# Adding one full-size product ahead of each set of 27-row products in the merging of the feed-forward weights

## The reference, cut to what matters

```python
gh = relu(einsum('bsd,hd->bsh', x, gfc1_w) + gfc1_b)
g = (einsum('bsh,eh->bse', gh, gfc2_w) + gfc2_b).mean(axis=1)   # 32 samples x 8
W1m = W1 + einsum('be,efd->bfd', g, tv_W1)                      # 32 x 512 x 128
W2m = W2 + einsum('be,edf->bdf', g, tv_W2)                      # 32 x 128 x 512
h = relu(einsum('bsd,bfd->bsf', x, W1m) + b1m[:, None, :])
out = einsum('bsf,bdf->bsd', h, W2m) + b2m[:, None, :]
```

## Time and profile before

| | |
|---|---|
| median of 3 runs | 759.09 us (758.73 to 762.13) |
| the profiled execution | 757.8 us, its span 755.8 us |
| busy, share of the span | TensorE 84%, weight loads 72%, VectorE 68%, ScalarE 58%, GpSimd 43% |
| mean granted TensorE clock | 0.912 of full speed |
| the merging, first to last product | 143.7 to 180.1 us |

### The profile page before, as it was taken

How to read it: one execution, slowest core, us unless ns; L and a number is a source line. 1 busy time by engine, 2 the same in 40 slices (tenths; PEclk the granted TensorE clock), 3 DMA queues, 4 the chain that set the end, 5 groups by cost and what they waited for, 6 DMA issues and landing times.

```text
span 755.8 us, 17403 instructions
## 1 busy us (share of the span) xinstructions
PE 637.0 (84%) x5635; PEld 540.7 (72%) x5635; DVE 511.3 (68%) x1393; ACT 437.7 (58%) x1176; POOL 322.4 (43%) x505
## 2 busy tenths in 40 slices
PE   4798989899999767999999898863789999999800
PEld 1357986799999334888888787753779988888700
DVE  5545653655555793578888887883787888878614
ACT  4485437645887647777776775622546666666500
POOL 0200000011565332122245578578874276777741
PEclk9999999855999888699999999995899999999955
DMA  8400000151000999940000000000023578788547
GB/s 254 137 1 1 2 2 1 36 159 36 0 0 0 310 343 358 335 121 3 2 3 2 20 26 29 17 30 28 32 76 108 207 273 290 273 292 281 192 143 260
DMA packets 58293, 88.52 MB, mean 117 GB/s; under 512 B 5974, under 2 KB 41651, under 8 KB 58228
## 3 DMA queue, kind: packets, MB, share of 16 engines
q1 hardware_dynamic: 48660, 74.78, 29.8%
q0 software_dynamic: 5344, 10.80, 4.5%
q10 hardware_dynamic: 4224, 2.10, 0.9%
HBM read 26.08 MB, written 37.19 MB: 84 GB/s over the span
## 4 chain that ended last, share of the span: by engine, by line
PE 48%; DVE 18%; ACT 14%; issue 8%; POOL 6%; DMA 3%; SPq 1%; DVEq 0%; POOLq 0%; ACTq 0%
DVE h_f L1875 4%; PE ps L1052 3%; PE ps3b L1092 3%; POOL rows_by_expert L766 3%; ACT h_s L1380 2%; PE ps L987 2%; PE ps L965 2%; PE ps3a L1079 2%; PE ps3a L987 2%; PE ps3b L997 2%; PE ps3a L997 2%; DVE hT L651 2%; PE ps3b L965 2%; ACT h_hi L1383 2%; PE ps3a L1120 2%
## 5 line engine op out<-in xcount | busy, mean ns | idle before, releaser
L796 POOL DMA_INDIRECT rows_by_token<-yrow,homei x93 | 95.0, 1021 | 55.8 <-issue 28.1
L1383 ACT CAST h_hi<-h_f 128x384 fp32r<-128x384 f32 x86 | 44.2, 514 | 75.6 <-DVE h_f L1875 69.4
L1332 ACT ACTIVATE arena<-ps3a,arena 128x141 f32<-128x141 f32 x192 | 55.6, 389 | 8.5 <-DVE arena L1759 7.9
L1898 DVE TENSOR_TENSOR h_lo<-h_f,h_hi 128x384 fp32r<-128x384 f32 x86 | 48.4, 562 | 16.6 <-ACT h_hi L1383 15.2
L685 POOL COPY wst<-arena 128x512 f32 (+1 forms) x32 | 36.0, 1128 | 41.2 <-DVE arena L1527 15.3
L1735 DVE RECIPROCAL arena<-ps 128x141 f32<-128x141 f32 x32 | 33.3, 1041 | 19.3 <-PE ps L1055 19.3
L1314 ACT ACTIVATE arena<-ps,vec,cst 128x141 f32<-128x141 f32 x32 | 15.1, 471 | 51.6 <-PE ps L1070 46.8
L1759 DVE TENSOR_REDUCE arena<-ps3a 128x2 f32<-128x282 f32 x96 | 38.5, 441 | 9.5 <-PE ps3a L1079 9.4
L766 POOL DMA_INDIRECT rows_by_expert<-xr,m_at x36 | 35.7, 991 | 11.0 <-issue 11.0
L766 POOL DMA_INDIRECT rows_by_expert<-xn,m_at x32 | 33.5, 1048 | 8.3 <-issue 8.3
L965 PE MATMUL ps3a<-gblk,tvc 27*128 27x96 f32 x262 | 36.3, 411 | 0.0
(11 more groups left out here) (405 smaller groups left out, 2336.9 us busy)
## 6 DMA issues: line engine op xcount, KB each, us to landing
rows_by_expert<-zeros SPq DMA_DIRECT2D x1, 18915.0 KB, 60.1
wb<-wparts SPq DMA_DIRECT2D x31, 512.0 KB, 3.2
wb<-wparts SPq DMA_DIRECT2D x31, 256.0 KB, 3.2
xrow<-rows_by_expert SPq DMA_DIRECT2D x31, 195.0 KB
tvc<-merge_rows SPq DMA_DIRECT2D x18, 320.0 KB, 3.1
rows_by_token<-zeros SPq DMA_DIRECT2D x2, 2304.0 KB, 43.8
ysum<-rows_by_token SPq DMA_DIRECT2D x10, 320.0 KB, 5.7
arena<-patches SPq DMA_DIRECT2D x4, 512.0 KB, 9.3
```

Of the source, the lines that this page charges most:

```text
L796: pool.indirect_dma_start(yt[:, :], bass.IndirectOffsetOnAxis(ap=homei[:, q, s:s + 1], axis=0), yrow[:, q, s, :], None, oob_is_err=True).t ...
L1332: ins = act.activation(b_e[:, q, h, :], bank[2 + i][:, (h % 2) * N:(h % 2) * N + N], ACT.Exp, bias=b_nm[:, q, h:h + 1])
L1383: act.copy(h_hi[:, s, 0:n], h_f[:, s, 0:n]).then_inc(S("h_hi"), 1)
L1898: dve.tensor_tensor(h_lo[:, s, :], h_f[:, s, :], h_hi[:, s, :].bitcast(F32), ALU.subtract).then_inc(S("h_lo"), 1)
```

## The change

Before the products of each set, TensorE now makes one more product, from `centre` (128 by 128) and the first 128 columns of `xn`, into the first bank of the four that the set then overwrites. Its columns 0 to 127 are overwritten by the set's own products, since these begin anew in the bank (start=True), for all but the last set; that set writes columns 0 to 95 and only these are read. The value is used nowhere. It is done 18 times, behind the waits for the eviction and ahead of the wait for the set's load.

```diff
                 mm.then_inc(S("mg_mm"), 1)
+            def keep_running(h, n):
+                pe.matmul(bank[4 * h][:, 0:n], C("centre"), chunk(xn, 0, n), start=True, stop=True, skip_group_check=True)
             for s in range(SETS):
                 if s == 1:
                     pe.wait_ge(S("bm_copied"), 1)
                 if s >= 2:
                     pe.wait_ge(S("mg_act"), s - 1)
                     pe.wait_ge(S("mg_dve"), s - 1)
+                keep_running(s % 2, P)
                 merge(s // 5, s % 5, s % 2)
```

## The result

The changed kernel takes 774.41 us (median of 4 runs, 773.94 to 777.60), the kernel before 758.98 us (median of 4, 758.73 to 762.13): a ratio of 1.0203, 95% interval 1.0164 to 1.0241. It is slower, clear of the noise; whether by more than 2% the interval leaves open. The profiled execution took 774.17 us, its span 772.2 us, 16.4 us over the span before. The forecast was 775.5 us, in a range of 764 to 780.

A forecast was written before the change was run, and what follows sets the result against it. The prediction took TensorE, busy throughout the stage at half clock, as the bound. Each added product costs 0.43 + 0.48 = 0.91 us, 18 of them +16.4 us on 759.09, giving 775.5 us, range 764 to 780.

The forecast's parts named there:

- TensorE alone sets the pace of the stage: In the stage of 27-row products TensorE is busy throughout, 35.66 of 35.66 us; evictions and loads are covered.
- The product itself, 0.43 us: Each added full-size product between sets takes two records of 0.214 us at 1.2 GHz.
- The changes of tiling, 0.48 us: Going from row groups to the whole array and back around each added product loses 0.48 us.
- the four places: Intervals into, within and out of full-size work in layer 1's first attention group, losing 0.14, 0.165, 0.165 and 0.12 us.
- 18 x 0.91 = 16.4 us: The 18 added products in the stage cost 0.91 us each, 16.4 us together; ends +7.7 and +18.4 us.
- The first one costs about as much as the others: The first added product, at about 143.7 us, fills the 0.74 us of full clock, so costs about 1 us.
- The clock stays at half: Through the stage the clock stays at 1.2 GHz; one large product in 3.04 us doesn't bring it back.
- The loop behind: The loop after the stage moves later, keeping its 3.65 us at half clock within a microsecond; counted as nothing.
- Rival 1: Added products bring the full clock back in the stage: 1.71 us a set, -8.3 us, 750.8 us; chance 0.12.
- Rival 2: The change of tiling in the stage is hidden under weight loads: +7.7 to +11 us, 767 to 770; chance 0.09.
- Rivals 3 and 4: In the stage: no change, product falls into a gap, chance 0.02; over 1.1 us each, above 780, chance 0.03.

The follow-up runs named there:

- e9: The changed kernel with 32 rows instead of 27 in the sets' products; sets 3.12 us apart, clock 0.5, ratio 1.0237 to the kernel before.
- e3: The changed kernel with the added products streaming 8 columns instead of 128; sets 2.92 us apart, ratio 1.0166 to the kernel before.
- e4: The changed kernel with two full-size products ahead of each set instead of one; sets 3.55 us apart, ratio 1.0336 to the kernel before.
- e5: The changed kernel with four 27-row products, one per row group, in place of each full-size one; sets 2.56 us apart, ratio 1.0091 to the kernel before.
- e10: The kernel before, unedited, traced on a chip of the experiments; sets 2.133 us apart, clock 0.5, stretch 41.45 us.
- e11: The changed kernel, unedited, on the same chip as e10; sets 3.12 us apart, stretch 58.26 us, ratio 1.0207 to the kernel before.
- e7: The kernel before with 32 rows instead of 27 in the sets' products, nothing added; sets 1.42 us apart at full clock, ratio 0.9834.
- e2: The changed kernel plus three full-size products in TensorE's waits ahead of the stage; sets 1.72 us apart, clock 1.0, ratio 0.9893 to the kernel before.
- e1: The kernel before plus three full-size products in TensorE's waits ahead of the stage, none in the sets; sets 1.43 us apart, clock 1.0, ratio 0.9842.
- e6: The changed kernel with its 18 products in one block ahead of set 2; sets 1.45 us apart behind it, ratio 0.9856 to the kernel before.

## Why the prediction was right

The direction, the mechanism and the size held. By its steps:

- *TensorE alone sets the pace of the stage.* Shown: TensorE is busy for all of the stage in the change and in e9, and what its own timeline shows for an added product (0.43 + 0.56 us in the change, 0.77 in e3) is, within 0.02 us, what the evictions came apart by, with nothing hidden.
- *The product itself, 0.43 us.* Shown by e4 and e5, each +0.43.
- *The changes of tiling, 0.48 us.* 0.56 measured. Of the four places only the first round behind the product was right, 0.11 us. For the way in I had cut the 0.40 us of the earlier trace rows by 0.075 for the shorter products; it shrank to 0.37, so 0.16 is lost and not 0.11. The pair loses 0.29 where 0.12 + 0.14 was taken; the 0.12 came from a pair whose weights have 104 columns instead of 128, which may be the reason but was not tried by itself. The way of working it out, from a similar sequence at the same clock, gave 0.91 for 0.987.
- *18 x 0.91 = 16.4 us.* The stretch grew by 17.05 us, the span by 16.4, the medians by 774.41 - 758.98 = 15.4. Each product costs 0.08 us more than forecast, 1.3 us for 17 of them, and the last one costs 0.28 instead of 0.91, because it lies under the last evictions; the prediction had counted all 18 alike. That the sum meets the span to the tenth owes something to luck: 0.65 us of the stretch's growth was given back elsewhere, 0.29 of it ahead of the stage, where the coefficients were written earlier.
- *The first one costs about as much as the others*, since it uses up the stretch of full clock. Set 0's eviction came 0.69 us later in the trace while the coefficients were written 0.29 us earlier (142.95 for 143.24): 0.98 us. On the chip of e10 and e11 it was less: from the coefficients to set 0's eviction 4.04 us for 3.30, 0.74 us. So this step holds roughly, and not in every run.
- *The clock stays at half.* Right in the change, and in e3, e4, e5, e9 and e11. The argument for it, that a stretch with more large products didn't have its clock back for 17 us, came to the right answer by weighing the wrong thing, how many large products there are. e7 has none and gets the clock back; e9 has 18 and doesn't, e4 has 36 and doesn't. That the clock stayed low was forecast rightly, but partly by luck.
- *The loop behind.* 3.6 us at half clock for 3.65, taken as no change, and none.
- *Rival 1* is what e2 shows once the clock is kept by other means: 1.72 us a set for 1.71, the stage 29.8 us for 29.9. The stretch is 8.3 us shorter, the rival's sum also says 8.3; the two cover different parts of the loop, so that they are equal is chance. *Rival 2*, the change hidden under the weight loads, is out: those have gaps now. *Rivals 3 and 4* didn't occur.

What the clock answers to is settled in part. Shown are: at the full clock 27 rows keep it (e1); at half clock 27 rows don't bring it back, 32 do (e7); a block of full-size products does (e6); one or two between sets don't, one with 27 rows or 32 (the change, e9), two with 27 (e4). So neither TensorE's busy time nor the number of large products decides, and the rows of the small products matter. Whether each row counts, or whether only a row group filled to its 32 rows differs, is open: nothing between 27 and 32 was tried. Why the added product keeps the clock low in e9 is open too; the 0.56 us lost around it may be the reason, but no run separates them from the rest.

The Trainium skill (TensorE: Matmul & The Clock Gate, Part 1) speaks of how busy the engine is. These runs disagree if that means the busy time of the trace: it is 6.90 of 6.90 us just ahead of the clock's return in e7 and 52.00 of 52.00 in e9 without one. The Trainium skill (TensorEngine Tiling, Key Properties) has a drain at a change of tiling mode. These runs agree: the change against e4 and e5 puts 0.56 us at 1.2 GHz on the way in and out together.

## What to carry to other kernels

Where TensorE is busy all the time at half clock, first ask what let the clock fall, and put products into the idle time there, where they cost next to nothing (in e1 0.07 us: from the gate's own first product to the coefficients it took 1.50 us, before 1.43); a filler between row-tiled products costs its own time, and the way in and out of the tiling on top, here 0.99 us for 0.43 us of work. Before adding anything, see whether the products can use more rows of the array: five rows of zeros in each group of 32 were worth 1.7% here. A filler that is meant to raise the clock can keep it low (e9 against e7), so read the granted clock in the stretch and not the busy time.

## What the runs showed of the hardware that I had not expected

- Products of 32 rows on four row groups, five of the rows zeros, brought the clock from 1.2 to 2.4 GHz in 6.9 us; the same products of 27 rows didn't in 35.66 us. The pace at half clock is the same, 2.14 us for the one set that e7 shows and 2.13 before.
- A full-size product of 8 columns between row-grouped ones costs 0.79 us at 1.2 GHz, one of 128 columns 0.99: most of the price isn't streaming.
- At the full clock the same added product moves the sets only from 1.43 us apart (e1) to 1.72 (e2), 0.29 us, though it takes about 0.58 us of TensorE's time (an estimate: 1.72 less ten rounds of 0.114 us). The rest lies in time in which TensorE waits for the evictions in e1: busy 22.82 of 25.50 us there, 31.10 of 32.00 in e2.
